# Transposing DMAs turn the probabilities from unit 50 on, not from unit 58, and feed-forward products use idle banks near the end of attention

## What is computed

```python
qkv = einsum('ble,ef->blf', layernorm(x), W_qkv)        # 16 heads of 32
q, k = rope(q), rope(k)
mask = (j <= i) & (j >= i - 128)                        # a band of 129 keys
attn = softmax(where(mask, q @ k.T / sqrt(32), min))
x = x + layernorm((attn @ v) @ W_out + b_out)
up, gate = h @ tern(W_up).T, h @ tern(W_gate).T         # h = layernorm(x); 2048 wide
x = x + layernorm((silu(up) * gate) @ tern(W_down).T)
# tern(w) = clip(round(w / s), -1, 1) * s, s = mean(|w|)
```

## Time and profile before

| | us |
|---|---|
| median of 3 runs | 1314.13 |
| lowest, highest | 1311.85, 1314.37 |
| the profiled execution | 1313.75 |
| its span in the profile | 1311.6 |
| TensorE busy in it | 1282.4 (98%) |
| VectorE, ScalarE, GpSimd busy | 929.6, 788.9, 705.5 |

### The profile page before, as it was taken

The page is one execution under the profiler, slowest core; times in us unless marked ns, Lnnn a source line. Parts: engine busy times, 40 slices in busy tenths (PEclk is TensorE's granted clock), DMA queues, the critical chain, the costliest instruction groups (busy, mean ns, idle before and its releaser), DMA issues.

```text
span 1311.6 us, 28139 instructions
## 1 busy us (share of the span) xinstructions
PE 1282.4 (98%) x9860; PEld 904.0 (69%) x9860; DVE 929.6 (71%) x2421; ACT 788.9 (60%) x1468; POOL 705.5 (54%) x957
## 2 busy tenths in 40 slices
PE   9799999999999999999999999999999999999997
PEld 6576767767677766767677676777667677666775
DVE  7687987876788767876778767887778767644333
ACT  3798987766566656656565664666556556533332
POOL 2476777555655546645555556555466354425432
PEclk9899999999999999999999999999999999999999
DMA  6856648767787567776588676785667646511010
GB/s 230 261 185 185 187 119 167 154 112 157 144 158 150 112 133 151 170 135 136 127 172 168 113 157 141 155 162 115 151 124 157 137 97 111 117 33 25 25 17 33
DMA packets 387276, 176.43 MB, mean 135 GB/s; under 512 B 314048, under 2 KB 366528, under 8 KB 387136
## 3 DMA queue, kind: packets, MB, share of 16 engines
q1 hardware_dynamic: 386272, 173.07, 60.9%
q10 hardware_dynamic: 864, 1.57, 0.4%
HBM read 71.76 MB, written 25.17 MB: 74 GB/s over the span
## 4 chain that ended last, share of the span: by engine, by line
PE 91%; DVE 3%; DMA 2%; ACT 2%; issue 1%; POOL 1%; SPq 0%; ACTq 0%; POOLq 0%; DVEq 0%
PE J L1637 29%; PE Y L1655 16%; PE J L1574 15%; PE J L1565 9%; PE J L1584 8%; PE S L1637 5%; PE O L1549 4%; PE S L1516 3%; PE Y L1524 1%; DMA Qp<-spill 1%; DMA spill<-split 1%; PE S L1513 1%; DVE room L1346 0%; ACT room L1097 0%; PE S L1512 0%
## 5 line engine op out<-in xcount | busy, mean ns | idle before, releaser
L1655 PE MATMUL Y<-down_q,room 128*128 128x512 fp8e4 x1024 | 262.2, 379 | 0.6 <-DVE room L1362 0.6
L1574 PE MATMUL J<-xnT,W 128*128 128x512 f32 x512 | 241.0, 596 | 0.9 <-ACT xnT L998 0.7
L1040 ACT ACTIVATE prob<-prob,peak 128x256 f32<-128x256 f32 (+1 forms) x512 | 226.3, 492 | 16.2 <-DVE peak L1292 16.0
L1292 DVE CUSTOM_DVE_ANT_0 prob<-S,band,neg_score_scale 128x256 f32<-128x256 f32 (+1 forms) x512 | 221.5, 470 | 9.2 <-PE S L1513 4.5
L1637 PE MATMUL J<-xT,gate_q 128*128 128x256 f16 x1760 | 210.2, 273 | 4.0 <-DVE room L1346 4.0
L1637 PE MATMUL J<-xT,up_q 128*128 128x256 f16 x1776 | 212.0, 273 | 0.0
L1637 PEld LDWEIGHTS J<-xT,gate_q 128*128 128x128 fp8e4 x1760 | 171.3, 98 | 49.4 <-DVE room L1346 8.6
L1097 ACT ACTIVATE room<-J,sig_scale 128x512 f32<-128x512 f32 x111 | 76.3, 687 | 214.0 <-PE J L1637 213.9
L1637 PEld LDWEIGHTS J<-xT,up_q 128*128 128x128 fp8e4 x1776 | 173.4, 98 | 43.8 <-DVE room L1356 1.6
L1346 DVE SCALAR_TENSOR_TENSOR room<-room,J 128x512 f32<-128x512 f32 x111 | 76.3, 687 | 175.1 <-ACT room L1097 175.0
L889 POOL TENSOR_TENSOR o_n<-o_raw,rinv 128x128 f32<-128x128 f32 x128 | 54.0, 422 | 266.7 <-DVE rinv L1321 266.5
(11 more groups left out here) (169 smaller groups left out, 1989.0 us busy)
## 6 DMA issues: line engine op xcount, KB each, us to landing
spill<-split SPq DMA_DIRECT2D x64, 256.0 KB, 2.5
Qp<-spill SPq DMA_DIRECT2D x127, 128.0 KB, 2.9
Kp<-spill SPq DMA_DIRECT2D x125, 128.0 KB, 2.9
x_in<-in_x SPq DMA_DIRECT2D x32, 256.0 KB, 3.1
X<-in_x SPq DMA_DIRECT2D x32, 256.0 KB, 3.5
out_x<-X SPq DMA_DIRECT2D x32, 256.0 KB, 3.3
turned<-parts SPq DMA_TRANSPOSE x198, 3.2
Kc<-Kp SPq DMA_DIRECT2D x24, 128.0 KB, 3.3
```

The costliest lines, as they stand in the source:

```text
L1040: e = nc.scalar.activation(prob[:, prob_home(U), a, begin:], prob[:, prob_home(U), a, begin:], ACT.Exp, bias=peak[:, prob_home(U), a:a + 1 ...
L1292: e = nc.vector.tensor_tensor_reduce(out=prob[:, prob_home(U), a, begin:], in0=S_ps[U % 2][:, a * 2 * P + begin:(a + 1) * 2 * P], in1=band ...
L1574: e = pe.matmul(dst[:], W[:, part, c, g * P:(g + 1) * P], xnT[:, c, :], start=(c == 0), stop=(c == DC - 1))
L1655: e = pe.matmul(Y_ps[t][:], h[:, q % HELD, part, (a * HT + t) * P:(a * HT + t + 1) * P], down_q[:, 2 * pair + a, :], start=(pair == 0 and ...
```

## The change

`BY_PE` becomes 50, so units 50 to 57 go the second way: no transposes on TensorE, `p_high` and `p_low` in slot U from prob to `parts`, one transposing DMA each on SP. `p_high` of units 50 and 51, which has no earlier turn to wait for, waits instead until the last weights that had their home in `parts` are cut.

Feed-forward products in slots 246 to 260 use J2, J0, J1 in turn, since no projection is in these banks then (`NO_JOBS` = 246, 264). The first in J0 and in J1 waits for the last projection there (`last_job`), and the first projection afterwards waits for the last feed-forward product in its bank (`ff_before`).

```diff
 FF_FIRST = 58
-BY_PE = FF_FIRST
+BY_PE = 50
...
+def slots_without_jobs():
+
+    used = [s for s in range(END) if pieces_at(s)]
+    gap = max(zip(used, used[1:]), key=lambda pair: (pair[1] - pair[0], pair[1]))
+    return gap[0] + 2, gap[1]
+
+
+NO_JOBS = slots_without_jobs()
...
-        if _s < TAIL:
+        if _s < NO_JOBS[0] or NO_JOBS[1] <= _s < TAIL:
             FF_BANK.append(2)
+        elif _s < TAIL:
+            FF_BANK.append([2, 0, 1][(_s - NO_JOBS[0]) % 3])
         else:
             FF_BANK.append([3, 4, 2][_n % 3])
...
+def last_job(bank, before):
+    return [j for n, j in enumerate(JOBS) if BANK[n] == bank and (j in PREPARED or ENDED[j] < before)][-1]
+
+
+def ff_before(job):
+
+    n = NUMBER[job]
+    if job in PREPARED or PRIOR[n] is None or not (ENDED[JOBS[PRIOR[n]]] if JOBS[PRIOR[n]] in ENDED else 0) < NO_JOBS[0] <= ENDED[job]:
+        return None
+    return [j for m, j in enumerate(FF_JOBS) if FF_BANK[m] == BANK[n]][-1]
...
                     k = U - PARTS
-                    if k >= BY_PE:
+                    if k < BY_PE:
+                        act.wait_ge(cut_done, 2 * (last_at_home(0) + 1))
+                    else:
                         act.wait_ge(p_turned[k % TURNED], 16 * ((k - BY_PE) // TURNED + 1))
...
                         emptied(pe, JOBS[PRIOR[n]])
+                    if ff_before((kind, g, tile)) is not None:
+                        ff_emptied(pe, ff_before((kind, g, tile)))
...
-                elif FF_BANK[n] == 2:
-                    emptied(pe, JOBS[max(m for m in range(len(JOBS)) if BANK[m] == 2)])
+                elif FF_BANK[n] <= 2:
+                    emptied(pe, last_job(FF_BANK[n], NO_JOBS[0]))
```

## The result

The changed kernel takes 1315.23 us (median of 20 runs, 1313.07 to 1317.75) against 1313.80 for the kernel before, run beside it 20 times. The ratio is 1.0013, 95% interval 1.0007 to 1.0019: by it slower by 1.7 us (0.9 to 2.5). That is inside 0.2%, but it is a loss, where I had forecast a gain of 1.8. The profiled execution took 1315.88 us, its span is 1313.7 (before 1313.75 and 1311.6, so +2.1).

A forecast was written before the change was run, and what follows sets the result against it. TensorE, busy 98% of the span, was taken as the bound. Banks at -4.4 and earlier transposing DMAs at +2.6 gave -1.8 us: 1312.0 in the profiled run's terms, 1312.3 for the median; range 1308.2 to 1316.0.

The forecast's parts named there:

- Part 2: Slots 246 to 260: three banks in turn remove the gate products' waits, -4.4 us, between -3.3 and -4.8.
- Part 1: Slots 50 to 58: transposes of units 50 to 57 go from TensorE to DMAs, +2.6 us, between +1 and +4.
- Moved copies: Slot 50 handles units 49 and 50: matmul behind `sum_halves` 0.6 us later, Q piece 0.45 later.
- (a): SP's queue, slot 51: K of group 3 stands behind unit 51's transposing DMA; score of unit 56 +1.4 us.
- From there TensorE gets back four groups: After the score of unit 56, four removed transpose groups of 0.47 us turn +1.4 into -0.5 at 199.27.
- rival D: Units 50 to 56: late landings of transposing DMAs hold `p_high`, +7.2 us, time 1316.9; chance 0.10.
- (b): SP's queue: turned feed-forward input xT stands behind unit 56's transposing DMA, delaying the first up product by 1.9 us.
- (c): `p_low` with two SBUF operands shares a port pair with GpSimd: 0.19 us for each of units 53 to 56, +0.8.
- all that is won or lost by the first up product comes out at the end unchanged: TensorE has no idle time from 300 to 1000 us, so the feed-forward start's gain or loss persists.
- rival C: Slots 246 to 261: `sum_halves` or logits become TensorE's wait, banks worth 1 us, time 1315.7; chance 0.12.
- Rival B: SP's queue costs nothing, `pack_k` and feed-forward input arrive in time: -8.2 us, 1305.9, partly true up to 1310.3; chance 0.18.
- 3.76 us of transposes: Slots 51 to 58: eight removed transpose groups of 0.47 us on TensorE, the most they can be worth beside waits.

The follow-up runs named there:

- e1: Changed kernel with transposing DMAs still beginning at unit 58, so only the three banks in slots 246 to 260 are new: 1310.39 us against 1313.61, ratio 0.9976.
- e2: Kernel before with only the earlier transposing DMAs added (BY_PE = 50), banks as before: 1319.05 us, ratio 1.0045 to the kernel before.
- e6: Changed kernel, but units 50 to 57 keep their probability copies and transposing DMA in slot U+1: ratio 1.0025 to the kernel before.
- e4: Changed kernel plus four unread identity transposes on TensorE (filler) in each of slots 51 to 58: ratio 1.0012 to the kernel before.
- e8: e5 with the cosine and sine table loads moved from slot 51 to slot 50: 1313.81 us, ratio 1.0002 to the kernel before.
- e9: e8 without the filler transposes on TensorE: 1314.46 us, ratio 1.0003 to the kernel before.
- e7: Changed kernel with BY_PE = 54, so only units 54 to 57 newly use transposing DMAs: 1313.46 us, ratio 0.9998 to the kernel before.
- e3: Changed kernel with SP's transposing DMAs of slots 50 to 57 moved to the end of their slot: ratio 1.0016 to the kernel before.
- e5: Changed kernel with the edits of both e3 and e4, transposing DMAs last in the slot and filler: ratio 1.0013 to the kernel before.
- e10: e8 with VectorE's `sum_halves` ahead of `p_low` in slots 50 and 56: 1314.68 us, ratio 1.0004 to the kernel before.
- e11: e10 without the filler transposes on TensorE: ratio 1.0003 to the kernel before.
- e12: e7 with the transposing DMAs moved to the end of their slot on SP: ratio 0.9992 to the kernel before.

## Why the prediction was wrong

**Part 2 was right.** Forecast -4.4, between -3.3 and -4.8; measured -4.33 in the kernel after and -3.4 to -4.3 in eleven others, by time -3.2 in e1. The gates' waits went, the one in slot 245 stayed (0.18), and VectorE gives back 0.7 where it shows at all.

**Part 1: the signs right, the size not.** Forecast +2.6, between +1 and +4; measured +6.2 in the trace (e2: +5.1 in its trace, +5.4 in time). Step by step, times of after less its late start of 0.2:

| step | forecast | measured |
|---|---|---|
| matmul behind `sum_halves` | 178.4 | 178.4 |
| Q piece | 182.5 | 182.6 |
| score of unit 56 | 186.8 | 187.7 |
| xT issued | 197.9 | 200.8 |
| xT landed | 201.1 | 205.2 |
| first up product | 202.0 | 205.5 |

- **Moved copies**: right to 0.1 us. e6 takes them back and gains the 0.6.
- **(a), K behind the turn**: the mechanism holds. The pack was issued at 182.88. Where the score visibly waits for K, it came 4.77 (e6), 4.85 (e2) and 5.07 us (e4) after the first pack; here that gives 187.65 to 187.95, and it stood at 187.90. I had allowed 4.3 for it (the median landing). By the prediction's own test, that this score must wait for its K, the kernel after fails, since the slow Q piece ends at the same moment. e4, e2 and e6 show the wait (1.59, 1.64 and 1.89).
- **"From there TensorE gets back four groups"**: this step failed. Between the score of unit 56 and the values products of slot 57 the distance grew by 1.30 us (3.56 less 2.26), where 1.4 for three groups should have come back. The step took it that only TensorE's own work counts there; what counted was `sum_halves`, 3.55 us later than before (199.59 less 0.22 against 195.82). One part of this is rival D's mechanism, a landing of 5.8 us where I had 3.2. I gave D 0.10 and let it act only if nearly every landing took over 5.5 us. One was enough to show, since it came where packs, tables and turns stood together, and VectorE behind it had no idle time left. But it is not the whole: moving the tables gave back 1.1 to 1.2 us (e8, e9), and e7, with no late landing, has the same wait of 2.06 and a distance that grew by 0.93 where 1.4 should have come back. There VectorE's operations beside GpSimd's were long (1.43, 1.76 and 0.94 us). How the loss divides between VectorE's order, its longer operations and the landings stays open.
- **(b), xT behind the turn of unit 56**: right as a mechanism (a wait of 1.28 for xT), but with `ff_low` at 196.23, not 193.6, it was issued 2.9 us later than forecast. It then landed after 4.4 us, not 3.2. Less the 0.8 that I had added for (c), these two make the 3.5 us by which the first up product missed 202.0, within 0.3.
- **(c), the shared port**: `p_low` of the eight units took 0.68, 0.69, 0.68, 0.83, 0.69, 0.68, 0.95 and 0.68 us: 0.4 more than 8 x 0.685, where I had 0.8, and over 0.69 twice rather than three times. `ff_low` took 1.76, from 196.23 to 197.99, beside GpSimd's from 195.83 to 197.44 and 0.55 more. That is what the Trainium skill (SBUF — State Buffer, "SBUF: two separate sides") says of two such operations; the trace agrees.
- **Left out altogether: the clock.** 2.18 us in slot 53 (4.99 less 2.81) and 1.50 in slot 58 (3.38 less 1.88). My own sum implied the first wait: 0.93 + 0.6 + 0.47 for the group removed ahead of it is 2.0 us in slot 51, and 2.01 it was. I never asked what the clock does behind it. In this kernel both falls are covered, the first by K, which is late anyway (e4), the second by xT, for which TensorE still waited 1.28 us after the slow piece. A fall is paid where nothing covers it: the first up product of e3, e5 and e9 waits for nothing behind pieces of 3.52, 3.28 and 2.97 us.
- **From the values of slot 57 to the first up product** the distance grew by 2.65. TensorE spent it as 1.50 for the slow piece, 1.28 for xT, about 0.3 for values products at the low clock, less 0.47 for the removed group; but with the clock full it would have waited for xT that much longer.

That all that is won or lost by the first up product comes out at the end unchanged held in the kernel after (892.31 us in both) and failed in most variants: in e10 another 4.6 us were lost behind it. The measured 1315.23 lies in my range, to 1316.0, and near rival C's 1315.7, but that is luck: C's mechanism is out.

**Rival B** (the queue costs nothing) is out, and no mend tried here rescues it: with the turns last, the clock full up to slot 58 and `sum_halves` first (e10), part 1 still costs 5.7, and as much without the filler, where the clock fell once (e11); the least was 3.1, with four units (e12). All three pay for the turns being last. The 3.76 us of transposes were never won in any kernel here. What they left became waits for VectorE, ScalarE and landings, from slot 51 to slot 61. The Trainium skill (VectorE: DVE Perf Modes, "Rules for kernel authors") says to turn a 128x128 block on TensorE where the result may go to PSUM; the runs agree, since giving these up cost 6.2 us instead of saving 3.76. **Rival C** (part 2 worth 1) is out by e1.

The version to keep is e1: 1310.39 us, 0.24% below the kernel before (0.14 to 0.34).

What stays open: why part 2 is worth 4.3 in five kernels and 3.4 to 3.7 in seven. The five are those that have no transposes at all in slots 51 to 58, the seven have 16 or 32; how that reaches slot 244 the traces don't say. The trace of e10 looks worse than its time (+2.1 in the distances, +0.7 in the median) for plainer reasons: it reached slot 50 0.46 us earlier, and at 1315.37 it is one execution 0.7 above its median.

## What to carry to other kernels

Work taken from the busiest engine pays only where that engine is the limit: look for waits in the very slots first, and follow the ones behind the gain (here to slot 61) before booking it. A transfer's landing time is a distribution, and the one that comes behind a crowd in its queue counts, not the median; ask what has no slack behind it. Where two causes end at the same moment, undoing either shows nothing, so undo both before calling one harmless. Ask of each new wait of TensorE whether its clock falls behind it, and whether something else covers the fall. And a mend in one queue has its own price further on: look at the slots behind the one that it mends.

## What the hardware showed that I had not expected

- **The clock in a kernel whose TensorE is 98% busy.** The granted clock went from 1.00 to 0.50 behind waits of 2.00 to 2.92 us in the kernel after, e2, e3, e5, e7 and e9. The Q piece then takes 4.81 to 5.11 us instead of 2.81 (after, e3, e9), or 3.02 where the clock was back early in it (e2). Behind waits of 1.13 to 1.59 us in e4 and e8 it stayed at 1.00. One wait does not decide it: it stayed at 1.00 behind 2.06 us in e12 and 1.96 in e11, and in e11 it fell after four waits of 0.80, 0.35, 0.92 and 0.51 us in a row. In slot 61 it fell around waits of 0.85 and 1.43 in e10, and stayed behind 0.77 and 1.43 in e8.
- **Added work that costs nothing.** e8 has eight more groups of transposes than e9 and reaches the first up product 1.55 us earlier; the whole times do not differ clear of noise.
- **A transposing DMA behind packs.** One of 1.23 us of issue landed after 5.8 us (median of the kernel before 3.2), and the issue itself once held the queue for 2.88 us. With the table loads moved ahead of the packs (e8 against e5), the turns of units 51 and 52 landed after 3.3 and 3.4 us instead of 4.5 and 3.8.
